# Graph attention with packed edge masks, the largest score as a column, and one low pass

## The reference, cut to what matters

```python
h = jnp.maximum(_layernorm(x, axis=-1), 0.0)
Wh = jnp.einsum('bnf,fo->bno', h, W)
f1 = Wh @ a[:fout, 0]
f2 = Wh @ a[fout:, 0]
e = f1[:, :, None] + f2[:, None, :]
e = jnp.where(e >= 0, e, 0.2 * e)
attention = jnp.where(adj > 0, e, -9e15)
attention = jax.nn.softmax(attention, axis=1)
h_prime = jnp.einsum('bij,bjo->bio', attention, Wh)
return x + jax.nn.elu(h_prime)
```

## Time and profile before

| | us |
|---|---|
| median of 3 runs | 1006.8 (1006.44 to 1007.97) |
| the profiled execution | 1006.23 |
| its span, first to last instruction | 1004.4 |
| PE busy | 958.5 |
| ACT busy | 929.5 |
| DVE busy | 875.3 |
| POOL busy | 544.0 |

### The profile page before, as it was taken

How to read it: one execution, slowest core, us unless ns; L and a number is a source line. 1 busy time by engine, 2 the same in 40 slices (tenths; PEclk the granted TensorE clock), 3 DMA queues, 4 the chain that set the end, 5 groups by cost and what they waited for, 6 DMA issues and landing times. The chain is left out here.

```text
span 1004.4 us, 23981 instructions
## 1 busy us (share of the span) xinstructions
PE 958.5 (95%) x8988; PEld 835.2 (83%) x8988; DVE 875.3 (87%) x1261; ACT 929.5 (93%) x1472; POOL 544.0 (54%) x574
## 2 busy tenths in 40 slices
PE   8878999999999999999999999999999999999996
PEld 6656888898888888888888888888888888888886
DVE  7799988999899998899988998899988988798763
ACT  3799999999999999999999999999999999998983
POOL 5445543655545655655556565465565554555534
PEclk9999999999999999999999999999999999999999
DMA  9577657889969978888978987888996987889535
GB/s 222 89 100 116 99 100 119 153 152 161 165 115 164 166 141 157 134 160 158 168 132 137 168 156 148 140 152 152 160 168 114 163 148 125 160 116 147 96 73 168
DMA packets 199061, 142.13 MB, mean 142 GB/s; under 512 B 7329, under 2 KB 187809, under 8 KB 198946
## 3 DMA queue, kind: packets, MB, share of 16 engines
q0 software_dynamic: 140160, 81.80, 60.4%
q1 hardware_dynamic: 58786, 58.81, 19.6%
HBM read 176.16 MB, written 16.84 MB: 192 GB/s over the span
## 5 line engine op out<-in xcount | busy, mean ns | idle before, releaser
L696 DVE CUSTOM_DVE_ANT_0 prob<-tp,f_row 128x2048 f32<-128x2048 bf16 x128 | 292.1, 2282 | 10.5 <-DMA f_row<-f_scratch 10.5
L435 PE MATMUL acc_st<-v,stored 128*128 128x256 f16 x992 | 270.2, 272 | 9.2 <-ACT part L558 5.1
L437 PE MATMUL acc_st<-v,stored 128*128 128x256 f16 x992 | 270.3, 273 | 0.0
L436 PE MATMUL acc_st<-v,stored 128*128 128x256 f16 x992 | 270.3, 272 | 0.0
L530 ACT ACTIVATE prob<-prob,shift 128x2048 f32<-128x2048 f32 x128 | 256.5, 2004 | 9.9
L521 ACT ACTIVATE prob<-prob,f 128x2048 f32<-128x2048 f32 x128 | 255.6, 1997 | 0.0
L808 POOL TENSOR_TENSOR direct<-prob,inv 128x1024 f16<-128x1024 f32 x128 | 242.4, 1894 | 10.0
L802 POOL TENSOR_SCALAR small_total<-total 128x1 f32<-128x1 f32 x128 | 28.7, 224 | 401.9 <-ACT prob L530 401.9
L453 PE MATMUL acc<-v,direct 128*128 128x256 f16 x1024 | 231.4, 273 | 4.8 <-ACT z_direct L564 4.8
L455 PE MATMUL acc<-v,direct 128*128 128x256 f16 x1024 | 231.3, 273 | 0.0
L710 DVE SCALAR_TENSOR_TENSOR direct<-prob,inv,direct 128x1024 f16<-128x1024 f32 x128 | 163.1, 1274 | 23.3 <-POOL direct L808 22.3
(11 more groups left out here) (85 smaller groups left out, 1344.6 us busy)
## 6 DMA issues: line engine op xcount, KB each, us to landing
raw<-in_adj POOLq DMA_DIRECT2D x64, 1024.0 KB, 10.0
y<-in_x SPq DMA_DIRECT2D x64, 256.0 KB, 2.9
out<-y SPq DMA_DIRECT2D x64, 256.0 KB, 2.2
y<-elu POOLq DMA_DIRECT2D x56, 256.0 KB, 4.3
x_in<-in_x SPq DMA_DIRECT2D x108, 128.0 KB, 3.7
f_row<-f_scratch SPq DMA_DIRECT2D x31, 256.0 KB, 6.4
stored<-in_x SPq DMA_DIRECT2D x4, 512.0 KB, 5.9
f_scratch<-f_t SPq DMA_DIRECT2D x124, 0.5 KB
```

The source lines that it names most:

```text
L435: nc.tensor.matmul(bank[:, 0:FO], p_st[:, 0, rows], v_c[:, 0, :], start=(c == 0), stop=False)
L436: nc.tensor.matmul(bank[:, 0:FO], p_st[:, 0, rows], v_c[:, 1, :], start=False, stop=False)
L437: last = nc.tensor.matmul(bank[:, 0:FO], p_st[:, 1, rows], v_c[:, 0, :], start=False, stop=(c == G - 1))
L696: nc.vector.tensor_tensor_reduce(out=prob[:, c % 2, :], in0=tp_b, in1=f1_row[:, b % 2, :], scale=1.0, scalar=-3.0e38, op0=ALU.add, op1=ALU ...
```

## The change

- **Packed masks.** A mask element is now a byte, 192 or 0 (`neg_bytes`); two bytes form one bf16, so one set of 16 transposes turns the masks of a pair of chunks. Chunk 2q + t has the columns 256q + 2p + t on partition p, and the rows are loaded and kept in the order 256q + 2p + t too, in x, in the residual and in the output. The mask load becomes 512 KB, one for each half of the rows of a pair of chunks, in every step; `raw` has four buffers of half the size.
- **The score pass** reads the bytes of its chunk, every other byte of PSUM, and subtracts: f1 comes scaled by 2^-48, the result is scaled by -2^48.
- **The largest score is column 2048 of `prob`**, so L521 does its leaky ReLU too; L519 goes. The shift now waits for the whole of L521.
- **One low pass** of 2 x 1024 elements, behind both high halves, over one tile `split` that holds direct and stored halves; TensorE's direct low products and its stored blocks both wait for it.
- **Order.** VectorE makes mask s + 3 ahead of the low pass of s - 1 (at s = 0 masks 2 and 3). The epsilon pass moves from VectorE to GpSimd, right ahead of the root.

```diff
-        raw = sb("raw", [P, 2, C, 2 * P], BF16)
+        raw = sb("raw", [P, 4, G, 2 * P], BF16)
         neg = sb("neg", [P, 2, C, P], BF16)
+        neg_bytes = neg[:].rearrange("p b m j -> p b (m j)").bitcast(U8).rearrange("p b (t q j) -> p b t q j", t=2, q=G)
-        prob = sb("prob", [P, 2, N], F32)
-        direct = sb("direct", [P, 2, 2, HALF], F16)
-        stored = sb("stored", [P, 2, G, 2, HALF], F16)
+        prob = sb("prob", [P, 2, N + 2], F32)
+        split = sb("split", [P, 4 + 4 * G, HALF], F16)
...
+        def x_rows(c):
+            b, j = divmod(c, C)
+            q, t = divmod(j, 2)
+            return x[b, 2 * P * q:2 * P * (q + 1), :].rearrange("(p t) f -> t p f", t=2)[t]
+        def masks_at(s):
+            if s < 0:
+                return [s + 5] if s >= -5 and s < -3 else []
+            return [2, 3] if s == 0 else ([s + 3] if s + 3 < CH else [])
...
-            def transpose_mask(c):
-                pe.wait_ge(neg_ready, c + 1)
+            def transpose_masks(pair):
+                pe.wait_ge(neg_ready, 2 * pair + 2)
-                wait(pe, scores, c)
+                wait(pe, scores, 2 * pair)
                 for m in range(C):
-                    last = nc.tensor.transpose(tp_b[:, m * P:(m + 1) * P], neg[:, c % 2, m, :], ident_b[:])
+                    last = nc.tensor.transpose(tp_b[:, m * P:(m + 1) * P], neg[:, pair % 2, m % 2 * G + m // 2, :],
+                                               ident_b[:])
...
-                nc.scalar.activation(most[:, c % R:c % R + 1], top[:, c % R:c % R + 1], ACT.Prelu, bias=f2, alpha=ALPHA
-                                     ).then_inc(most_s, 1)
-                nc.scalar.activation(p, p, ACT.Prelu, bias=f2, alpha=ALPHA).then_inc(leaky, 1)
-                act.wait_ge(most_s, c + 1)
-                nc.scalar.activation(shift[:, c % R:c % R + 1], most[:, c % R:c % R + 1], ACT.Copy, scale=-1.0
+                nc.scalar.activation(p_top, p_top, ACT.Prelu, bias=f2, alpha=ALPHA).then_inc(leaky, 1)
+                act.wait_ge(leaky, c + 1)
+                nc.scalar.activation(shift[:, c % R:c % R + 1], prob[:, c % 2, N:N + 1], ACT.Copy, scale=-1.0
                                      ).then_inc(shift_s, 1)
...
-                nc.vector.tensor_scalar(neg[:, c % 2], raw[:, pair % 2, :, c % 2 * P:(c % 2 + 1) * P], 0.0, -NOT_AN_EDGE, ALU.is_le, ALU.mult
-                                        ).then_inc(neg_ready, 1)
+                nc.vector.tensor_scalar(neg_bytes[:, pair % 2, t], raw[:, n % 4], 0.0, NOT_AN_EDGE,
+                                        ALU.is_le, ALU.mult).then_inc(neg_ready, 1)
...
                 nc.vector.tensor_tensor_reduce(
-                    out=prob[:, c % 2, :], in0=tp_b, in1=f1_row[:, b % 2, :], scale=1.0, scalar=-3.0e38,
-                    op0=ALU.add, op1=ALU.max, accum_out=top[:, c % R:c % R + 1]).then_inc(scores, 1)
+                    out=prob[:, c % 2, 0:N], in0=tp_bytes[:, c % 2, :], in1=f1_row[:, b % 2, :], scale=-1.0 / F1_SCALE,
+                    scalar=-3.0e38, op0=ALU.subtract, op1=ALU.max, accum_out=prob[:, c % 2, N:N + 1]).then_inc(scores, 1)
...
                 dve.wait_ge(hi_direct, c + 1)
+                dve.wait_ge(hi_stored, c + 1)
                 wait(dve, direct_done, c - 1)
...
+                nc.vector.scalar_tensor_tensor(
+                    out=split[:, lo_d:lo_s + 1:lo_s - lo_d, :], in0=prob[:, c % 2, 0:N].rearrange("p (h c) -> p h c", h=2),
+                    scalar=inv[:, c % R:c % R + 1], in1=split[:, hi_d:hi_s + 1:hi_s - hi_d, :],
+                    op0=ALU.mult, op1=ALU.subtract).then_inc(lo_ready, 1)
...
+                for n in masks_at(s):
+                    make_masks(n)
                 if chunk(s - 1):
                     split_low(s - 1)
...
-                nc.gpsimd.dma_start(raw[:, pair % 2], adj[b].rearrange("(c p) j -> p c j", p=P)[
-                    :, :, 2 * P * q:2 * P * (q + 1)]).then_inc(raw_in[pair % 2], 16)
+                nc.gpsimd.dma_start(raw[:, n % 4], adj[b].rearrange("(q p t) j -> t p q j", p=P, t=2)[
+                    t, :, :, 2 * P * q:2 * P * (q + 1)]).then_inc(raw_in[n % 4], 16)
...
             def root(g):
+                rs = slice(4 * g % RS, 4 * g % RS + 4)
+                pool.wait_ge(mv_s, 4 * g + 4)
+                wait(pool, xn_ready, 4 * g + 4 - RS)
+                nc.gpsimd.tensor_scalar(var_eps[:, rs], mv[:, rs, 1], EPS, None, ALU.add).then_inc(var_s, 1)
                 pool.wait_ge(var_s, g + 1)
```

More of the change, by code:

```diff
@@ L16 @@
 EPS = 1e-5
-NOT_AN_EDGE = 2.0 ** 56
+F1_SCALE = 2.0 ** -48
+NOT_AN_EDGE = 192.0
 P_BITS = 14
@@ L84, in graph_attention @@
         w_a = prob[:, 1, 0:4 * FO].rearrange("p (i o) -> p i o", i=4)
-        spare = stored[:, 1].rearrange("p g h c -> p (g h c)").bitcast(F32).rearrange("p (i c) -> p i c", c=F)
+        spare = split[:, 4 + 2 * G:4 + 4 * G].rearrange("p s c -> p (s c)").bitcast(F32).rearrange("p (i c) -> p i c", c=F)
         x_early, xn_early, h_t_early = spare[:, 0:EARLY], spare[:, EARLY:EARLY + 4], spare[:, EARLY + 4:EARLY + 6]
@@ L181, in f2_col, with direct_slot, stored_slot @@
             return 64 + c % RF
+        def direct_slot(c, low):
+            return (10, 0)[c % 2] + low
+        def stored_slot(c, low):
+            return ((12, 2), (28, 20))[c // G % 2][c % 2] + 2 * (c % G // 2) + low
         def x_buf(c):
@@ L446, in direct_blocks @@
                     pe.wait_ge(f_ready, LEAD)
-                p_d = direct[:, c % 2]
+                p_hi, p_lo = split[:, direct_slot(c, 0), :], split[:, direct_slot(c, 1), :]
                 v_c = v[:, c % RV]
@@ L484, in _ @@
                     store_block(n)
-                if chunk(s + 1):
-                    transpose_mask(s + 1)
+                if chunk(s + 1) and s % 2 == 1:
+                    transpose_masks((s + 1) // 2)
                 if chunk(s + LEAD + 1):
@@ L526, in attention @@
                     take_direct(b - 1, 1)
-                act.wait_ge(leaky, c + 1)
                 act.wait_ge(shift_s, c + 1)
@@ L632, in multiply_w @@
                 nc.vector.tensor_tensor_reduce(
-                    out=w_a[:, i, :], in0=w_raw[:, k, :], in1=a_row[:, side, :], scale=1.0, scalar=0.0,
+                    out=w_a[:, i, :], in0=w_raw[:, k, :], in1=a_row[:, side, :], scale=(F1_SCALE, 1.0)[side], scalar=0.0,
                     op0=ALU.mult, op1=ALU.add, accum_out=w_cat[:, k, FO + side:FO + side + 1]).then_inc(w_ready, 1)
@@ L666, in aggregate @@
                 nc.vector.bn_aggr(mv[:, c % RS, :], stats[:, c % 2, :]).then_inc(mv_s, 1)
-            def add_eps(g):
-                dve.wait_ge(mv_s, 4 * g + 4)
-                wait(dve, rstd_s, g - RS // 4 + 1)
-                rs = slice(4 * g % RS, 4 * g % RS + 4)
-                nc.vector.tensor_scalar(var_eps[:, rs], mv[:, rs, 1], EPS, None, ALU.add).then_inc(var_s, 1)
             def make_offset(g):
@@ L763, in _ @@
                     multiply_w(3)
-                if s == -5:
-                    make_mask(0)
-                if s == -4:
-                    make_mask(1)
-                if chunk(s + 2) and s >= 0:
-                    make_mask(s + 2)
                 for k in finish(s - 1):
@@ L803, in split_high @@
                 pool.wait_ge(total_s, c + 1)
-                wait(pool, lo_stored, c - R + 1)
+                wait(pool, lo_ready, c - R + 1)
                 nc.gpsimd.tensor_tensor(k, t, minus_one[:], ALU.pow).then_inc(inv_ready, 1)
@@ L836, in _ @@
                     finish_add(k)
-                if s % 2 == 0 and s >= 0 and chunk(s + 4):
-                    load_raw(s // 2 + 2)
+                if s >= -1 and chunk(s + 5):
+                    load_raw(s + 5)
                 if chunk(s + LEAD + 2) and s < 0:
                     normalise(s + LEAD + 2)
-                if s == -16:
-                    load_raw(0)
-                if s == -12:
-                    load_raw(1)
+                if s in (-16, -15, -12, -11):
+                    load_raw((-16, -15, -12, -11).index(s))
                 if root_at(s) is not None:
```

84 lines of the change are left out of this document (36 added, 48 removed).

## The result

The changed kernel takes 1038.06 us (median of 4 runs, 1037.36 to 1039.28) against 1006.63: ratio 1.0311, 95% interval 1.0293 to 1.0328. Forecast: 1036. The profiled execution has a span of 1035.6 (before 1004.4).

What follows compares the result with a forecast made beforehand. ScalarE was taken to set the step, VectorE's chain the lengthened ones. Six batches at +4.6 give +28, batch 0 +1, last batch -1, prologue +1: +29, so 1036 us; range 1016 to 1062, allowed 1006 to 1066.

Steps and rivals of the forecast that it cites:

- batch 0: First batch, no finish: four roots at about +0.9, twelve steps at -0.07, -2 from TensorE; +1 us in all.
- the last batch: Batch without roots and with x work done: -1 us.
- the prologue: Two masks made in the prologue, 0.53 us each: +1 us.
- ScalarE sets the step: ScalarE bounds most steps; L519 gone, shift waiting for L521: its step gets 0.07 us shorter, bounds 0 to 0.10.
- Masks 1.22, low pass 2.34, score pass unchanged: VectorE's pass times in us: masks 1.22 (686 ns before), one low pass 2.34, score pass 2.28 unchanged.
- the two rivals on these prices: Masks at one element at a time, 2.28 us: 1105, chance 0.07; score pass slower by half: 1110 or more, 0.03.
- Steps 4, 8 and 12: Root waits out the low pass, VectorE's offset waits for it: 8.97, 8.6, 8.0 us, so +1.05, +1.75, +1.15.
- Step 0: Root ends at 5.0, GpSimd starts the inverse 0.5 us late, ScalarE's stored half waits: +0.4 on 7.84.
- Step 6: VectorE's chain with elu and half sum, masks starting at 0.8: 7.5 us against 6.89, +0.6.
- The spare 0.5 covers it: TensorE's direct low matmuls wait for the whole low pass; 0.5 us a chunk from halved transposes covers that.
- ScalarE's waits for the score: Profile sign: ScalarE waits for VectorE's score some 30 us in all, against 6.5 before.
- The upper bound: 1062 us: masks lose to GpSimd's next instruction in steps 4 and 7, epsilon costs a whole low pass, +0.5 x 4.

Runs made afterwards that it cites:

- E5: Kernel before the change with only the largest score as a column of the leaky pass, the shift waiting for it: 998.4 us, ratio 0.9919.
- E9: Changed kernel, epsilon on VectorE, masks behind the low pass, offset behind the next score, x normalised on GpSimd in ScalarE's long steps: 995.9 us, ratio 0.9891.
- E1: Changed kernel with the epsilon pass back on VectorE and nothing else: 1016.8 us.
- E2: Changed kernel with the masks moved behind the low pass and the offset: 1034.9 us.
- E7: Changed kernel with epsilon on VectorE, masks behind the low halves and two low passes: 1011.4 us, ratio 1.0046.

## Why the prediction was right, and where it was not

*The total.* 1036 forecast, 1038.1 measured. The fifth batch grew by 4.45 against 4.6, but the six batches by 25.7 against 28, and the other parts by more than forecast: batch 0 1.9 against 1, the last batch 1.1 against -1, the prologue 2.5 against 1. The steady part is understood; that the total is within 2 us is in part luck, as these errors offset each other.

*ScalarE sets the step, and gains 0.07.* Right. The nine steps where only ScalarE counts went from 69.1 to 68.5, and E5 gave 8.4 us for the column alone (998.4 against 1006.7 beside it) against 8. One part of the run is an exception: in the kernel before, steps 11 to 14 of batch 0 (7.23 to 7.24) end in a wait of ScalarE for TensorE, 0.29 us each.

*Masks 1.22, low pass 2.34, score pass unchanged.* 1.218, 2.340 and 2.282. For the masks the middle value between two far ends was the right one; the two rivals on these prices fell. The load's issue was put at 1.1 and has a median of 0.99.

*The root.* Steps 4, 8 and 12 were put at 8.97, 8.6 and 8.0, and came at 8.82, 8.48 and 7.94, with the root ending 0.91 after the low pass. (For step 12 the forecast's own terms, 4.0 + 0.90 + 0.08, give 4.98 and not 5.05.) The behaviour read from two rows before the change (a GpSimd instruction ends 0.9 after the pass it met) carried these three. The Trainium skill (SBUF — State Buffer, SBUF: two separate sides) gives it as an exclusive lock for a whole instruction. In part the traces agree: in E9 a GpSimd pass of 0.56 us was held for a whole low pass and took 2.66. In part they do not: in E1 the last 0.90 of the root ran beside a low pass that was none the longer, 2.33; and who got the turn did not follow the recorded starts alone, as in E9 the pass that was issued 0.04 us earlier was the one that waited.

*Step 0, mis-sized.* +0.4 forecast, +0.67 measured. Held back to 4.97 by the root, GpSimd's inverse then met the elu pass and took 0.84 in place of 0.57; the chain of holds has one more link than I counted.

*Step 6.* 7.5 forecast, 7.55 measured.

*Batch 0, too small, and the last batch, wrong in sign.* Batch 0 came at +1.9 where +1 was forecast, with 2 us of relief for TensorE in it. The roots cost about what was forecast (0.85, 1.02 and 0.60 in steps 4, 8 and 12, nothing in step 0). What failed is "twelve steps at -0.07". Once a root has made VectorE late, it asks for its masks 0.75 into the step and meets the load's issue, every step anew. One such step in batch 0, which starts at 73.74, GpSimd first:

```profile
74.14 0.98 POOL L800 DMA_DIRECT2D raw<-in_adj  x1
```

And VectorE:

```profile
74.48 1.66 DVE L698 TENSOR_SCALAR neg<-raw 128x2048 uint8<-128x2048 bf16 x1
76.07 2.33 DVE L724 SCALAR_TENSOR_TENSOR split<-prob,inv,split 128x2048 f16<-128x2048 f32 x1
```

The mask pass took 1.66, and the step 7.14 in place of 6.75. With the masks behind the low pass (E2) such steps took 6.75 and batch 0 111.4; that batch 0 has 1.7 to gain from the packing is E7's.

The last batch was put at -1 and came at +1.1. Most of that is its step 1, 8.10 against 7.31: VectorE is ahead there and runs a mask pass beside GpSimd's inverse, which takes 1.39 in place of 0.57, and ScalarE waits 1.83 for it. With the masks behind the low pass (E2) that step took 7.28, but others got longer and the batch did not get shorter.

*TensorE's wait for the whole low pass.* "The spare 0.5 covers it": the time was covered (E2), the size was not foreseen: 81.7 us of new waits.

*ScalarE's waits for the score* were forecast at some 30 us and are 15. The rest of the loss is in its wait for the inverse, 41.9 in all where the profile before had 17.0: I had seen that path in step 0 only.

*The upper bound.* The terms named for it, 7 us for the masks and 0.5 for each of some 28 roots, add up to 21 us above 1036, so 1057 and not 1062.

*Prologue.* +2.5 against +1. The first leaky pass starts between 36.3 and 40.5 us over all the kernels run; what sets it was not tried.

## What to carry to other kernels

Before moving a small pass onto an engine that looks idle, ask what it will stand behind there, who waits for its result, and what is queued behind that waiter: here 0.2 us of work moved cost 21 us. Fewer and longer passes are not free where a second engine gets its turn only between them. And a packing that halves a part of one engine's work pays only where that engine sets the step; here TensorE was 95% busy by the page and set only the last steps of batch 0.

## What the runs showed of the hardware that I had not expected

- A GpSimd instruction already waiting when a VectorE pass ends gets through before the next pass counts against it (E1: root issued 573.73, ended 0.90 after the masks, inside the low pass). But one issued 0.04 us before a low pass, while the short v low pass was just ending, was held for all of it (E9: 2.66 us for 0.56, 13 times); issued 0.15 us or more before, it took 0.56.
- The issue of a mask load on GpSimd holds and is held: 0.98 us for 512 KB when free (1.27 for 1024 KB in the earlier trace rows, so halving the bytes saves little), and up to 2.32 beside a mask pass; a mask pass of 1.22 took 1.66 beside such an issue.
- The score pass read every other byte of PSUM at the same 2282 ns as it read 16-bit elements.
